# Second pass of expert tiles: the finish moved one turn later, and three list groups marked ahead of the loop

## The chip, the cores and the metric

The kernel runs on one core of a Trainium2 chip. The metric is the device time of one execution in microseconds (us). Engines: TensorE (PE, with its weight loads PEld), VectorE (DVE), ScalarE (ACT), GpSimd (POOL), SyncE (SP); DMA queues are fed by SP and POOL.

## The reference

Cross-attention of 4096 tokens of width 512 on a context of 3202 rows (16 heads), a residual, and then a layer of 8 experts of which each token uses 2. All in float32. The part that matters here:

```
x = x + attention(layernorm(x), ctx, ctx, Wq, bq, Wk, bk, Wv, bv, Wo, bo)
h = layernorm(x)
p = softmax(h @ W_router.T + b_router)            # 4096 x 8
w, e = top_k(p, 2)                                # two experts a token, with weights
x = x + sum over j in (0, 1) of  w[:, j] * (h @ W_experts[e[:, j]].T + b_experts[e[:, j]])
```

## The kernel before

Attention and the router take the first 2055 us of the profiled execution; the change is in what follows, the function mix_experts. The residual rows stand in a DRAM table, token_rows, of 4096 rows with two halves of 516 floats: the near half holds the row, its layernorm scale and shift and the two weights, the far half takes the result of the first pass.

The tokens are sorted by expert into tiles of 128 rows, once by their first expert and once by their second. There are NS = 39 tiles in each of the K = 2 passes, so NT2 = 78 tiles in one loop; tile s is in pass k = s // 39, at place n = s % 39. The rows of a tile all go through one expert, so a tile is one product of 128 x 512 by 512 x 512 in three terms (high and low parts). Since 39 tiles allow for eight partly filled ones, the last tiles of a pass may be short or empty; rows that are left out are skipped by the transfer's bounds.

**The lists.** Which row stands where is found by small products: mark_tiles and mark_lanes (VectorE, L1972 and L1977) mark for a group of four columns of tokens their tile and lane, in two buffers by turns, and find (TensorE, L2081) multiplies them into a bank of PSUM, four matmuls a group. A pass has NGR = 8 groups. The first pass's are done ahead of the loop. The second pass's are done inside it, one group every three turns, and index(1) (L1985 to L1990), which turns them into row numbers, is in turn 28.

**The loop.** Each engine runs its own list of instructions in order; semaphores order them among each other. For tile s:

- GpSimd: scatter(s) waits for finish(s), then writes the result, in pass 0 to the far half of the table (L1898), in pass 1 to the output (L1902). Behind it gather(s + 6) loads the rows of a later tile into one of HOLD = 6 buffers hold: in pass 0 and for the first six tiles of pass 1 the near half alone (L1886), for the others both halves, 128 rows of 4128 bytes (L1890). As a buffer is used again every six tiles, gather(s + 6) waits for finish(s). For the first six tiles of pass 1 the far half is loaded by gather_far (L1910), once every scatter of pass 0 has landed; two of them stand behind the last scatter of pass 0, one behind each gather after that.
- ScalarE: in its iteration s, normal(s + 3) (L1935), which waits for the gather, and behind it high(s + 2) (L1942), which waits for the turned tile.
- TensorE: multiply(s) (L2103), then turn(s + 2) (L2089, four transposes), then in some turns find.
- VectorE: biased(s) (L2003) adds the bias to multiply's result, low(s + 2) (L1994) makes the low part, finish(s) (L2012) multiplies by the weight and adds the rows of hold (near half in pass 0, far half in pass 1), then marks. multiply(s) needs low(s) and high(s). biased(s) needs a free result buffer of RES = 3, so a landed scatter(s - 3).

These are the waits by which the rings turn:

```
pool.wait_ge(final_done, s - HOLD + 1)                 # gather(s)
act.wait_ge(near_in[s % HOLD], 16 * times_used(HOLD, s))  # normal(s)
dve.wait_ge(xh_done, s + 1)                            # low(s), after high(s)
dve.wait_ge(far_in[n], 16)                             # finish(s) in pass 1, n < HOLD
```

Of the kernel before, what the change touches and what calls it, by code (L numbers as in the profile page):

```python
# [1789 lines left out]
def mix_experts(nc, mem, sb0, sem, psum, ident, g, h):  # L1790
    D, KT, NE, L, out = (g[n] for n in "D KT NE L out".split())
    NTL, K, NS, table, we_hi, we_lo, picked, before, mix = (h[n] for n in "NTL K NS table we_hi we_lo picked before mix".split())
    lane, own, mix_stored = (h[n] for n in "lane own mix_stored".split())
    wo = g["wo"]
    G4 = 4
    NGR = NTL // G4
    HOLD, RES = 6, 3
    AHEAD = 2
    MARKS_OVER = 3
    FAR_FIRST = 2  # L1800
    RANK_BANK, COUNT_BANK, PLACE_BANK, T_BANK = 0, 1, 2, 4
    OUT_BANKS = (6, 7, 0, 1)
# [2 lines left out]
    NT2 = K * NS  # L1805
    NSE = NS + NS % 2

    with mem:
# [57 lines left out]
        with nc.Block() as block:  # L1866
# [7 lines left out]
            def _(pool):  # L1874
                def gather(s):
                    k, n = kn(s)
                    if s >= HOLD:
                        pool.wait_ge(final_done, s - HOLD + 1)
                    else:
                        pool.wait_ge(counted, 4 + s + 1)  # L1880
                    if s == 0 or n == 0:
                        pool.wait_ge(indexed, k + 1)
                    if s == 0:
                        pool.wait_ge(mix_stored, 16 * NGR)
                    if k == 0 or n < HOLD:
                        pool.indirect_dma_start(out=hold[s % HOLD][:, 0:ROW], out_offset=None, in_=halves[:, :],  # L1886
                                                in_offset=bass.IndirectOffsetOnAxis(ap=near[k][:, n:n + 1], axis=0),
                                                bounds_check=2 * L - 1, oob_is_err=False).then_inc(near_in[s % HOLD], 16)
                    else:
                        pool.indirect_dma_start(out=hold[s % HOLD][:, :], out_offset=None, in_=table[:, :],  # L1890
                                                in_offset=bass.IndirectOffsetOnAxis(ap=whole[:, n:n + 1], axis=0),
                                                bounds_check=L - 1, oob_is_err=False).then_inc(near_in[s % HOLD], 16)
# [16 lines left out]
                def gather_far(n):  # L1909
                    pool.indirect_dma_start(out=hold[(NS + n) % HOLD][:, ROW:2 * ROW], out_offset=None, in_=halves[:, :],  # L1910
                                            in_offset=bass.IndirectOffsetOnAxis(ap=far[1][:, n:n + 1], axis=0),
                                            bounds_check=2 * L - 1, oob_is_err=False).then_inc(far_in[n], 16)

                for s in range(NT2):
                    scatter(s)
                    if s == NS - 1:
                        for b in range(RES):
                            pool.wait_ge(scattered[b], 16 * len(range(b, NS, RES)))
                        for n in range(FAR_FIRST):
                            gather_far(n)  # L1920
                    if s + HOLD < NT2:
                        gather(s + HOLD)
                    if NS - 1 <= s < NS - 1 + HOLD - FAR_FIRST:
                        gather_far(s - (NS - 1) + FAR_FIRST)
                for b in range(RES):
# [33 lines left out]
            def _(dve):  # L1959
                c = h["chained"]  # L1960

                def step(ins):
                    c[0] += 1
                    ins.then_inc(chain, 1)
                    dve.wait_ge(chain, c[0])
# [16 lines left out]
                def index(k):  # L1982
                    dve.wait_ge(placed, RANKED + (k + 1) * NTL)
                    found = psum[:, PLACE_BANK + k, 0:NS]
                    step(dve.tensor_scalar(gone[:], found, 0.0, SKIPPED, ALU.is_equal, ALU.mult))  # L1985
                    step(dve.scalar_tensor_tensor(out=row_of[:], in0=found, scalar=-1.0, in1=gone[:], op0=ALU.add, op1=ALU.add))
                    if k:
                        step(dve.tensor_copy(whole[:], row_of[:]))
                    dve.tensor_scalar(near[k][:], row_of[:], 2.0, None, ALU.mult).then_inc(indexed, 1)
                    step(dve.tensor_scalar(far[k][:], row_of[:], 2.0, 1.0, ALU.mult, ALU.add))  # L1990
# [15 lines left out]
                def finish(s):  # L2006
                    k, n = kn(s)
                    if k and n < HOLD:
                        dve.wait_ge(far_in[n], 16)
                    dve.wait_ge(bias_done, s + 1)  # L2010
                    rest = hold[s % HOLD][:, ROW:ROW + D] if k else hold[s % HOLD][:, 0:D]
                    dve.scalar_tensor_tensor(out=res[s % RES][:, 0:D], in0=res[s % RES][:, 0:D], scalar=hold[s % HOLD][:, MIX_AT + k:MIX_AT + k + 1], in1=rest,  # L2012
                                             op0=ALU.mult, op1=ALU.add).then_inc(final_done, 1)
# [40 lines left out]
                step(dve.tensor_scalar(expert[:], expert_f[:], float(NE - 1), None, ALU.min))  # L2054
                dve.sem_inc(rankable, 1)
                dve.wait_ge(be_in, 16 * NE)

                for s in range(AHEAD):
                    low(s)
                for s in range(NT2):  # L2060
                    biased(s)
                    if s + AHEAD < NT2:
                        low(s + AHEAD)
                    finish(s)
                    for part in range(s * (G4 + 1) // MARKS_OVER, min((s + 1) * (G4 + 1) // MARKS_OVER, NGR * (G4 + 1))):
                        q, u = divmod(part, G4 + 1)
                        if u == 0:
                            mark_tiles(1, q)
                        else:
                            mark_lanes(1, q, u - 1)  # L2070
                    if s == MARKS_OVER * (NGR + 1) + 1:
                        index(1)

            @block.tensor
            def _(pe):
                def find(k, q):
                    m = k * NGR + q
                    pe.wait_ge(marked, 2 * (m + 1))
                    for u in range(G4):
                        i = q * G4 + u  # L2080
                        pe.matmul(psum[:, PLACE_BANK + k, 0:NSE], at_lane[m % 2][:, u, :], at_tile[m % 2][:, u, :],  # L2081
                                  start=i == 0, stop=i == NTL - 1).then_inc(placed, 1)

                def turn(s):
                    pe.wait_ge(xs_done, s + 1)
                    if s >= 2:
                        pe.wait_ge(xl_done, s - 1)
                    for k in range(KT):
                        mm = pe.transpose(psum[:, T_BANK + s % 2, k * P:(k + 1) * P], xs[s % 2][:, k * P:(k + 1) * P], ident[:])  # L2089
                    mm.then_inc(xs_turned, 1)  # L2090

                def expert_of(s):
                    k, n = kn(s)
                    return pe.value_load(expert[0:1, k, n:n + 1], min_val=0, max_val=NE - 1)

                def multiply(s, e):
                    pe.wait_ge(xh_done, s + 1)
                    pe.wait_ge(xl_done, s + 1)
                    if s >= 4:
                        pe.wait_ge(bias_done, s - 3)  # L2100
                    terms = [(k, A, W) for k in range(KT) for A, W in ((x_hi, we_hi), (x_hi, we_lo), (x_lo, we_hi))]
                    for t, (k, A, W) in enumerate(terms):
                        mm = pe.matmul(psum[:, OUT_BANKS[s % 4], :], A[s % 2][:, k, :], W[:, k, ds(e, 1), :].rearrange("p o n -> p (o n)"),  # L2103
                                       start=t == 0, stop=t == len(terms) - 1)
                    mm.then_inc(e_mm, 1)

                pe.wait_ge(rankable, 2)
                pe.matmul(psum[:, COUNT_BANK, 0:K * NE], all_ones, before[:, NTL].rearrange("p k e -> p (k e)"), start=True, stop=True).then_inc(ranked, 1)
                pe.matmul(psum[:, RANK_BANK, :], earlier, picked[:].rearrange("p i k e -> p (i k e)"), start=True, stop=False)
                pe.matmul(psum[:, RANK_BANK, :], all_ones, before[:, 0:NTL].rearrange("p i k e -> p (i k e)"), start=False, stop=True).then_inc(ranked, 1)  # L2110
                for q in range(NGR):
                    find(0, q)
                pe.wait_ge(rankable, 3)
                for s in range(AHEAD):
                    turn(s)
                for s in range(NT2):
                    e = expert_of(s)
                    multiply(s, e)
                    if s + AHEAD < NT2:
                        turn(s + AHEAD)  # L2120
                    if s >= MARKS_OVER + 2 and (s - 2) % MARKS_OVER == 0 and (s - 2) // MARKS_OVER <= NGR:
                        find(1, (s - 2) // MARKS_OVER - 1)


_DRAM = ["x", "ctxT", "Wq", "bq", "Wk", "bk", "Wv", "bv", "Wo", "bo", "WeT", "be", "WrT", "br"]
# [29 lines left out]
```

## Time and profile before

| | us |
|---|---|
| median of 3 runs | 2355.64 (2354.8 to 2356.03) |
| the profiled execution, its time | 2361.31 |
| the profiled execution, its span | 2358.5 |
| TensorE busy over the span | 2266.8 (96%) |
| VectorE busy | 2035.5 (86%) |
| ScalarE busy | 1840.5 (78%) |
| GpSimd busy | 746.6 (32%) |
| first multiply of the expert loop starts | 2081.91 |
| last scatter starts | 2349.52 |

The expert loop is the last 11% of the span, so the shares over the whole span say little about it; the rows below are from its own stretch.

### The profile page before, as it was taken

What the parts mean: (1) busy time and instruction counts of PE and PEld (TensorE: products, weight loads), DVE (VectorE), ACT (ScalarE), POOL (GpSimd) and SP (SyncE); (2) the same over time, 40 slices, a digit from 0 to 9 for tenths busy, and PEclk for the clock granted to TensorE, in tenths of its full rate; (3) what the DMA queues carried; (4) which work ended last, traced back from release to release, by engine and by line L of the source; (5) the groups of instructions that cost most, each with busy time, mean ns of one, the idle gap of its engine ahead of it and who ended that gap; (6) DMA issues with size and microseconds to landing.
All of it is one profiled execution on the core that took longest, in us unless ns stands there. A gap on an engine that the chain in (4) does not pass through costs nothing. (4 is left out here: it accounts for less than half of the span.)

```text
span 2358.5 us, 49254 instructions
## 1 busy us (share of the span) xinstructions
PE 2266.8 (96%) x19600; PEld 1088.8 (46%) x19600; DVE 2035.5 (86%) x1830; ACT 1840.5 (78%) x2123; POOL 746.6 (32%) x823
## 2 busy tenths in 40 slices
PE   8999799999999999999999999999999999789998
PEld 7878533333333333333333333333333357578776
DVE  4358579999999999999999999999999988866555
ACT  3213299999999999999999999999999956534332
POOL 2213223323223322223323232332233222245664
PEclk9999899999999999999999999999999999889999
DMA  7436463444464455557444535645434467634463
GB/s 261 166 133 224 171 184 91 109 107 107 113 175 108 127 127 131 130 140 208 109 109 115 120 92 129 170 100 120 109 95 106 109 171 267 201 112 139 144 215 120
DMA packets 145020, 334.24 MB, mean 142 GB/s; under 512 B 32758, under 2 KB 65494, under 8 KB 127644
## 3 DMA queue, kind: packets, MB, share of 16 engines
q0 software_dynamic: 47104, 194.30, 33.8%
q1 hardware_dynamic: 95356, 129.20, 16.8%
q10 hardware_dynamic: 2336, 7.60, 1.0%
q8 instruction: 159, 2.61, 0.4%
q14 instruction: 65, 0.53, 0.1%
HBM read 131.16 MB, written 82.78 MB: 91 GB/s over the span
## 5 line engine op out<-in xcount | busy, mean ns | idle before, releaser
L1162 ACT ACTIVATE probs<-psum 128x1536 f32<-128x1536 f32 x800 | 1159.5, 1449 | 0.0
L1316 PE MATMUL psum<-probs,v_st 128*32 128x512 f32 x6400 | 853.9, 606 | 0.2 <-ACT probs L1162 0.2
L1267 PE MATMUL psum<-q_st,k_st 32*128 32x512 f32 x9600 | 781.2, 426 | 28.6 <-ACT probs L1162 13.6
L1267 PEld LDWEIGHTS psum<-q_st,k_st 32*128 32x128 f32 x9600 | 399.0, 184 | 722.8 <-ACT probs L1161 376.3
L1227 DVE TENSOR_TENSOR even_sums<-even_sums,probs 128x2048 f32<-128x2048 f32 x288 | 659.7, 2291 | 39.1 <-ACT probs L1162 36.2
L1227 DVE TENSOR_TENSOR odd_sums<-odd_sums,probs 128x2048 f32<-128x2048 f32 x256 | 585.4, 2287 | 1.6 <-ACT probs L1162 1.6
L1161 ACT ACTIVATE probs<-psum 128x512 f32<-128x512 f32 x800 | 478.2, 598 | 47.3 <-PE psum L1267 42.8
L1316 PEld LDWEIGHTS psum<-probs,v_st 128*32 128x32 f32 x6400 | 126.1, 108 | 291.3 <-issue 281.9
L2103 PE MATMUL psum<-we_hi,wo 128*128 x624 | 216.9, 409 | 4.5 <-DVE wo L1994 2.5
L977 POOL DMA_DIRECT2D pile<-probs x96 | 88.8, 925 | 247.2 <-DMA pile<-probs 156.7
L956 POOL CAST rest_split<-rest_probs 72x512 fp32r<-72x512 f32 x32 | 37.4, 1169 | 386.1 <-ACT rest_probs L1130 386.1
L971 POOL DMA_DIRECT2D pile<-rest_probs x128 | 103.6, 1222 | 149.3 <-DMA pile<-probs 149.3
L1935 ACT ACTIVATE shared_rows<-hold 128x512 f32<-128x512 f32 x78 | 63.5, 814 | 102.3 <-DMA hold<-token_rows,whole 62.4
L2103 PEld LDWEIGHTS psum<-we_hi,wo 128*128 128x128 f32 x624 | 118.2, 189 | 31.5 <-issue 6.3
L344 POOL TENSOR_TENSOR squares<-o_hi 128x512 fp32r<-128x512 f32 (+1 forms) x60 | 60.5, 1017 | 208.3 <-ACT o_hi L382 121.0
L2103 PE MATMUL psum<-we_lo,wo 128*128 x312 | 123.7, 397 | 0.0
L1227 DVE TENSOR_TENSOR even_sums<-probs 128x2048 f32<-128x2048 f32 x32 | 105.7, 3302 | 12.2 <-ACT probs L1162 12.2
L1942 ACT ACTIVATE wo<-psum 128x512 fp32r<-128x512 f32 x78 | 46.0, 590 | 75.5 <-PE psum L2089 75.5
L958 POOL TENSOR_TENSOR rest_split<-rest_probs,rest_split 8x512 fp32r<-8x512 f32 x32 | 100.5, 3141 | 2.7
L1994 DVE TENSOR_TENSOR wo<-psum,wo 128x512 fp32r<-128x512 f32 x78 | 53.9, 691 | 53.2 <-ACT wo L1942 53.1
L762 PE MATMUL psum<-wo,q_st 128*128 128x512 f32 x384 | 96.4, 400 | 0.0
L786 POOL DMA_DIRECT2D shared_rows<-inv_scratch x124 | 61.8, 506 | 88.7 <-DMA inv_scratch<-spread_inv 88.7
(225 smaller groups left out, 2358.9 us busy)
## 6 DMA issues: line engine op xcount, KB each, us to landing
pile<-probs POOLq DMA_DIRECT2D x128, 1024.0 KB, 7.3
token_rows<-rows SPq DMA_DIRECT2D x8, 1028.0 KB, 6.7
xn<-in_x SPq DMA_DIRECT2D x16, 512.0 KB, 6.4
qh_scratch<-o_hi SPq DMA_DIRECT2D x8, 1024.0 KB, 4.5
ql_scratch<-o_lo SPq DMA_DIRECT2D x8, 1024.0 KB, 7.6
q_st<-qh_scratch SPq DMA_DIRECT2D x32, 256.0 KB, 3.0
q_st<-ql_scratch SPq DMA_DIRECT2D x32, 256.0 KB, 3.6
token_rows<-in_x SPq DMA_DIRECT2D x8, 1024.0 KB, 10.7
```

The source lines that it names most:

```text
L762: mm = pe.matmul(psum[:, bank, :], A[:, j, :], W[:, j, :], start=False, stop=t == len(terms) - 1)
L786: pool.dma_start(a["recip"][h * DH:(h + 1) * DH, :], a["inv_d"][h:h + 1, :].to_broadcast([DH, CH])).then_inc(a["inv_in"], 16)
L958: pool.tensor_tensor(rest_split[DH:DH + REST, :], rest_probs[DH:DH + REST, :], rest_split[DH:DH + REST, :].bitcast(F32), ALU.subtract).the ...
L971: pool.dma_start(out=pile[rows, h, :], in_=rest_probs[rows, :], accum_op=ALU.add).then_inc(piled, 16)
L977: pool.dma_start(out=pile[:], in_=probs[:, p_slot(it, t)], accum_op=ALU.add).then_inc(piled, 16)
L1161: act.activation(probs[:, p, 0, :], psum[:, FIRST_BANK, :], ACT.Exp, bias=-WIDEST, scale=SCALE).then_inc(first_done, 1)
L1162: act.activation(probs[:, p, 1:HG, :], psum[:, bank(it, t, 1):bank(it, t, 1) + HG - 1, :], ACT.Exp, bias=-WIDEST, scale=SCALE).then_inc(ex ...
L1227: nc.vector.tensor_tensor(into[:], a, probs[:, p_slot(it, t)], ALU.add).then_inc(added, 1)
L1267: return nc.tensor.matmul(psum[:, bank(it, t, h), :], k_st[rows, part, t * P:(t + 1) * P], q_st[it % 2][rows, of, :], start=start, stop=stop)
L1316: mm = nc.tensor.matmul(psum[h * DH:(h + 1) * DH, bank, :], lhs(h), rhs(h), start=start, stop=stop)
L1935: act.activation(xs[s % 2], r[:, 0:D], ACT.Identity, bias=r[:, SHIFT_AT:SHIFT_AT + 1], scale=r[:, RSTD_AT:RSTD_AT + 1]).then_inc(xs_done, 1)
L2103: mm = pe.matmul(psum[:, OUT_BANKS[s % 4], :], A[s % 2][:, k, :], W[:, k, ds(e, 1), :].rearrange("p o n -> p (o n)"), start=t == 0, stop=t ...
```

## The change

In the first pass VectorE's order within a turn stays biased(s), low(s + 2), finish(s). In turn 39, the first of the second pass, it does no finish, and from turn 40 on it does finish(s - 1); the last tile's finish stands behind the loop. Three of the second pass's eight list groups are marked, and their products done, ahead of the loop, between the expert numbers and the first low or turn; the other five follow inside the loop from turn 0 on, and index(1) moves from turn 28 to turn 19.

```diff
+    EARLY_GROUPS = 3
...
                 dve.wait_ge(be_in, 16 * NE)
+                for q in range(EARLY_GROUPS):
+                    mark_tiles(1, q)
+                    for u in range(G4):
+                        mark_lanes(1, q, u)
...
                     if s + AHEAD < NT2:
                         low(s + AHEAD)
-                    finish(s)
-                    for part in range(s * (G4 + 1) // MARKS_OVER, min((s + 1) * (G4 + 1) // MARKS_OVER, NGR * (G4 + 1))):
-                        q, u = divmod(part, G4 + 1)
+                    if s < NS:
+                        finish(s)
+                    elif s > NS:
+                        finish(s - 1)
+                    for part in range(s * (G4 + 1) // MARKS_OVER, min((s + 1) * (G4 + 1) // MARKS_OVER, (NGR - EARLY_GROUPS) * (G4 + 1))):
+                        q, u = divmod(part + EARLY_GROUPS * (G4 + 1), G4 + 1)
...
-                    if s == MARKS_OVER * (NGR + 1) + 1:
+                    if s == MARKS_OVER * (NGR - EARLY_GROUPS + 1) + 1:
                         index(1)
+                finish(NT2 - 1)
...
                 pe.wait_ge(rankable, 3)
+                for q in range(EARLY_GROUPS):
+                    find(1, q)
                 for s in range(AHEAD):
                     turn(s)
...
-                    if s >= MARKS_OVER + 2 and (s - 2) % MARKS_OVER == 0 and (s - 2) // MARKS_OVER <= NGR:
-                        find(1, (s - 2) // MARKS_OVER - 1)
+                    if s >= MARKS_OVER + 2 and (s - 2) % MARKS_OVER == 0 and (s - 2) // MARKS_OVER <= NGR - EARLY_GROUPS:
+                        find(1, EARLY_GROUPS + (s - 2) // MARKS_OVER - 1)
```

## Rows read from the trace of the kernel before

**Rows 1.** Windows: stretch, length, each engine's busy time, granted clock, DMA share, GB/s.

```profile
2063.00:2073.00 10.00, 8.35 (x32) 7.43 (x32) 8.86 (x37) 0.00 (x0) 0.00 (x0) 0.50 0.24 90
2079.00:2082.00 3.00, 2.29 (x9) 1.52 (x9) 0.69 (x1) 2.41 (x4) 2.39 (x3) 0.50 0.52 119
2223.00:2230.00 7.00, 5.25 (x28) 4.09 (x27) 5.27 (x8) 1.30 (x2) 5.47 (x6) 1.00 0.67 207
2242.00:2246.00 4.00, 2.78 (x14) 1.78 (x12) 0.64 (x2) 1.30 (x2) 2.42 (x3) 1.00 0.84 276
2246.00:2300.00 54.00, 53.33 (x260) 43.23 (x261) 33.35 (x51) 21.42 (x33) 32.59 (x32) 1.00 0.67 209
```

**Rows 2.** Chain that ended last, in two stretches of the loop: start, length, what.

```profile
2100.24 2.81 PE psum L2103 x12
2103.84 2.90 PE psum L2103 x12
...
2286.28 2.81 PE psum L2103 x12
2289.52 2.81 PE psum L2103 x12
```

**Rows 3.** Timeline at the border of the passes: finish(39), multiply(42), low(44).

```profile
2223.13 0.75 DVE L2012 SCALAR_TENSOR_TENSOR shared_rows<-shared_rows,hold 128x512 f32<-128x512 f32 x1 [4.57 <-DMA hold<-token_rows,far]
...
2225.45 0.49 PE L2103 MATMUL psum<-we_hi,wo 128*128 x1 [1.75 <-issue]
...
2232.26 0.69 DVE L1994 TENSOR_TENSOR wo<-psum,wo 128x512 fp32r<-128x512 f32 x1 [2.90 <-ACT wo L1942]
```

**Rows 4.** Timeline of the second pass: one round from finish(45) to finish(48), then finish(60).

```profile
2246.05 0.74 DVE L2012 SCALAR_TENSOR_TENSOR shared_rows<-shared_rows,hold 128x512 f32<-128x512 f32 x1
...
2247.62 1.00 POOL L1902 DMA_INDIRECT out<-shared_rows,whole  x1 [2.59 <-DVE shared_rows L2012]
...
2248.93 1.03 POOL L1890 DMA_INDIRECT hold<-token_rows,whole  x1 [0.30 <-issue]
...
2253.26 0.82 ACT L1935 ACTIVATE shared_rows<-hold 128x512 f32<-128x512 f32 x1 [2.81 <-DMA hold<-token_rows,whole]
...
2253.99 0.58 ACT L1942 ACTIVATE wo<-psum 128x512 fp32r<-128x512 f32 x1
...
2254.59 0.69 DVE L1994 TENSOR_TENSOR wo<-psum,wo 128x512 fp32r<-128x512 f32 x1 [1.14 <-ACT wo L1942]
...
2255.20 0.74 DVE L2012 SCALAR_TENSOR_TENSOR shared_rows<-shared_rows,hold 128x512 f32<-128x512 f32 x1
...
2295.21 0.74 DVE L2012 SCALAR_TENSOR_TENSOR shared_rows<-shared_rows,hold 128x512 f32<-128x512 f32 x1
```

**Rows 5.** Line L1890, all 33 gathers; timeline: gather(77) and normal(77).

```profile
DMA to landing us min/median/max: 2.1/4.6/5.9
...
2333.04 1.03 POOL L1890 DMA_INDIRECT hold<-token_rows,whole  x1 [0.30 <-issue]
...
2335.52 0.81 ACT L1935 ACTIVATE shared_rows<-hold 128x512 f32<-128x512 f32 x1
```

**Rows 6.** Timeline ahead of the loop: marks and matmuls of pass 0, expert numbers, turn(0).

```profile
2061.67 0.33 DVE L1972 TENSOR_TENSOR wo<-lane,tile_of 128x160 fp32r<-128x160 f32 x1
...
2062.94 0.32 DVE L1972 TENSOR_TENSOR wo<-lane,tile_of 128x160 fp32r<-128x160 f32 x1
...
2063.07 1.04 PE L2081 MATMUL psum<-wo 128*128 128x40 f32 x4 [5.70 <-DVE wo L1977]
...
2075.77 0.19 DVE L2054 TENSOR_SCALAR expert<-expert_f 1x78 int32<-1x78 f32 x1
...
2079.05 1.09 PE L2089 MATMUL psum<-ident,shared_rows 128*128 128x128 f32 x4 [6.10 <-ACT shared_rows L1935]
```

**Rows 7.** Timeline at the end: first matmul of multiply(76), and scatter(77).

```profile
2341.24 0.48 PE L2103 MATMUL psum<-we_hi,wo 128*128 x1
...
2349.52 0.98 POOL L1902 DMA_INDIRECT out<-res,whole  x1 [1.82 <-DVE res L2012]
```

## The prediction

> **What bounds the kernel now.** The change touches only the expert stage, so I read the windows of that stage first, then the chain that ended last, then the timeline at three places: the start of the loop, the border between the two passes, and the steady part of the second pass. I write F(s), B(s), L(s), H(s), N(s), T(s), M(s) for finish, biased, low, high, normal, turn and multiply of tile s, S(s) and G(s) for its scatter and gather; tiles 39 to 77 are the second pass.
>
> The windows say that TensorE is the busiest engine in the loop: 53.33 of 54 us between 2246 and 2300, at full clock, against 33.35 for VectorE and 32.59 for GpSimd [rows 1]. The chain agrees: M to M takes 2289.52 - 2286.28 = 3.24 us, and a turn in the first pass that also holds a group of list matmuls takes 2103.84 - 2100.24 = 3.60, so one group costs 0.36 [rows 2]. The reader should see, though, that at the border the engine is not full: 5.25 of 7 us and 2.78 of 4 [rows 1]. There F(39) waits 4.57 us on VectorE for its far half, and TensorE shows an idle 1.75 us before M(42), because L(42) is queued behind F(39) [rows 3]. This is the wait that moving the finish goes at.
>
> The view that decides is none of the totals. It is one round through the ring of six row buffers. G(s+6) may start only after F(s), since it overwrites the rows that F(s) reads. N(s+6) waits for it to land. ScalarE issues N(s+6) ahead of H(s+5), so H(s+5) waits too; L(s+5) follows H(s+5). The timeline shows all of it for tile 45: F(45) 2246.05, S(45) 2247.62, G(51) 2248.93, N(51) 2253.26, H(50) 2253.99, L(50) 2254.59, and right behind it on VectorE F(48) 2255.20 [rows 4]. The steps are 1.57 + 1.31 + 4.33 + 0.73 + 0.60 + 0.61 = 9.15 us. In the order of before, L(50) and F(48) stand in the same turn, so a round carries the finishes three tiles on: 9.15 / 3 = 3.05 us a tile, only 0.19 under TensorE's 3.24. From F(45) to F(60), 15 tiles, it took 2295.21 - 2246.05 = 49.16, or 3.28 a tile [rows 4]. Two resources thus stand side by side, and TensorE's share of busy time hides the second.
>
> **The change, part by part.**
>
> *The finish one turn later.* In turn s of VectorE the order is now B(s), L(s+2), F(s-1). L(50) is in turn 48, and what stands behind it is F(47), not F(48). The round of 9.15 us, none of whose links is touched, now carries the finishes two tiles on: F(s+2) is at least F(s) + 9.15. That is 4.58 us a tile against 3.24, as two interleaved chains, even and odd. It is the late gather that is paid for: S(s), G(s+6) and everything behind them on GpSimd's queue wait a turn longer.
>
> Does anything cover it? TensorE needs 3.24 a tile and can't run ahead, as M(s+2) needs L(s+2). GpSimd needs S and G, 2 x 1.31 = 2.6. The wait of B(s) for the landed S(s-3) is the shorter path beside it, since the path through G also has the longer transfer. So nothing hides it while gathers are still to come, which means up to G(77), released by F(71) and ending in F(73).
>
> Where the rounds begin: at the border F(39) still waits for the same far gather until 2223.13, and GpSimd's three transfers a turn run as before, so L(44) stays near 2232.26 [rows 3]. I take F(41) = 2232.26 + 0.61 = 2232.87. M(42) may start earlier by the 1.75, but M(44) waits for L(44) all the same, so I cost this gain at nothing; if it were kept it would be -1.75. From F(41) to F(73) are 16 rounds: 16 x 9.2 = 147.2 (9.15 rounded up for the waits at GpSimd). The last gathered tile is short: G(77) starts 2333.04 and N(77) runs at 2335.52 without a wait, so 2.48 at most instead of 4.4 [rows 5], which takes off 1.9. F(73) = 2232.9 + 147.2 - 1.9 = 2378.2. L(76) stands 0.61 ahead of it, 2377.6, and M(76) 0.9 behind L(76) (0.69 of VectorE and some 0.2 until TensorE starts), 2378.5. Before, M(76) started at 2341.24 [rows 7]: +37.2 us. Behind it the tail is as before, but F(76) and F(77) are now back to back and S(77) queues behind S(76): one more slot of 1.31. Sum of this part: **+38.5**.
>
> The landing is the term that I know least. Over the 33 whole-row gathers it is 2.1 / 4.6 / 5.9 us, least, median, most [rows 5]; the round above has 4.33. With the median it would be 16 x 0.27 = 4.3 more. Against that, the queues carry one tile in 4.6 us rather than 3.24, so crowding eases. I take 4.33 to 4.4, that of a gather with no other right ahead of it, and keep -0.6 and +0.7 a round for the range (-10, +11).
>
> The Trainium skill, page "DMA: Bandwidth & Descriptors", section "Anatomy of one DMA — SWDGE (gpsimd) path", gives 2.0 us plus the bytes over 436 GB/s for such a transfer. For 128 rows of 4128 bytes this is an estimated 3.2 us, and by it this part would be near 16 x 1.13 = 18 us smaller; the row at 4.33 disagrees, and the sum goes by the row.
>
> *Three groups marked ahead of the loop.* The work on the expert numbers ends at 2075.77 + 0.19 + 0.04 = 2076.0. A group of marks takes 2062.94 - 2061.67 = 1.27 us, and its matmuls start 1.40 behind its first mark [rows 6]. The third group starts at 2078.54, its matmuls at 2079.94, and four of them took 1.04, so they end at about 2080.9. VectorE is free by 2079.9, in time for L(0). But T(0) started at 2079.05 [rows 6] and is queued behind these matmuls on TensorE: +1.85 at the start of the loop. The pause isn't as long as it looks from VectorE. In the loop three groups go, 3 x 0.36 = -1.07. VectorE has slack in those turns, and the earlier index(1) is needed by no one before tile 39; both nothing. Sum: **+0.8**. The clock bounds it: at 2079 to 2082 it is granted at 0.50, the 1.2 GHz level, and 8.35 us of work in 2063 to 2073 did not raise it [rows 1]. If the later start lets M(0) run more of its work at the 2.4 GHz level, up to 2 us come back; so +0.8, from -1.3 to +1.0.
>
> **Sum.** 38.5 + 0.8 = +39.3 us. The rows are from one execution with a span of 2358.5 us and a time of 2361.31; the median of the runs is 2355.64. On the median: 2355.64 + 39.3 = **2395 us**.
>
> **The rivals.**
>
> *The ring has slack, and the border's wait is saved.* If the ring were no limit, the result would be 1.85 - 1.07 - 1.75 = -1.0, so 2354.7; with the clock's 2 us back, 2352.7. For it speaks the full TensorE of 2246 to 2300. It decides if a round fits in two turns of TensorE, 2 x 3.24 = 6.49 us, so only if a gather landed in 4.33 - 2.66 = 1.67 us, under the least landing of 2.1 [rows 5]. Chance 0.05. It is the only case on the faster side, and even it stays mostly within 0.2% (4.7 us), about what a measurement of this kernel can tell.
>
> *The gathers land sooner once the queues are emptier.* Halfway between 2.48 and 4.33 the landing is 3.4, 0.93 less: 16 x 0.93 = 15, so 2380 us. Against it: gathers with little ahead of them, as G(51), still took 4.33. Chance 0.08. The page's 3.2 us above would give about 2377.
>
> *TensorE's clock falls.* It would be idle for 4.6 - 3.24 = 1.3 us a turn. At the lower level a turn would take 6.49, so 32 x (6.49 - 4.58) = 61 more: 2456. But at the border it was busy for 5.25 of 7 and 2.78 of 4 us, 70 to 75% and so much as it would be then (3.24 / 4.58 = 71%), and the clock stayed at 1.00 [rows 1]. Chance 0.05.
>
> *The forecast*, 2384 to 2408: chance 0.82. Its own bounds are 2395 - 10 - 2 = 2383 and 2395 + 11 = 2406; I widen the top by 2, for parity chains that meet at GpSimd. Leaving out the three rivals leaves out under 2 in 10, so that is the range. Faster 0.02, within 0.2% 0.04, slower 0.94.
>
> **What would show each step.** Right: in the timeline of the second pass F(s+2) - F(s) of about 9.2 us with L(s+5) just ahead of F(s+2), TensorE at some 70% from 2235 to 2380 and idle before its turns or multiplies with ScalarE's rows waiting for the whole-row gather; a gather after each scatter, a turn later than before; T(0) near 2080.9; 3.60 us turns five times, not eight; two scatters back to back at the end. Wrong: TensorE full in the second pass, or a landing well off 4.4 us, which scales the result sixteenfold; or a granted clock of 0.50 beyond tile 0.

## The result and the profile after

The changed kernel takes 2396.07 us (median of 5 runs, 2394.09 to 2396.74) against 2356.03 (5 runs, 2354.8 to 2359.08) of the kernel before beside it: 40.0 us more, a ratio of 1.0165 with a 95% interval of 1.0151 to 1.0178, which is 35.6 to 41.9 us. The prediction was +39.3 us.

The page of the changed kernel, its span and its first part (busy time and share of the span):

```profile
span 2392.7 us, 49254 instructions
PE 2279.1 (95%) x19600; PEld 1092.5 (46%) x19600; DVE 2034.0 (85%) x1830; ACT 1840.1 (77%) x2123; POOL 747.3 (31%) x823
```

No engine got more work: each runs as many instructions as before. VectorE, ScalarE and GpSimd are busy for the same time as before within 2 us. TensorE shows 12 us more for the same matmuls, since a multiply or a turn that starts after a pause takes longer (3.06 us in place of 2.81 for a multiply's twelve, see below). The loss is idle time, and nothing on this page says where. (The two spans differ by 34.2 us only, since the part ahead of the expert stage, which the change does not touch, was 4.1 us shorter in this execution. I compare from the operation on the expert numbers on.)

The windows of the changed kernel, columns as in [rows 1]:

```profile
2160.00:2210.00 50.00, 50.00 (x249) 40.75 (x248) 31.07 (x46) 21.50 (x31) 31.05 (x32) 1.00 0.40 127
2235.00:2380.00 145.00, 119.51 (x518) 86.67 (x516) 63.79 (x98) 40.79 (x63) 64.61 (x63) 0.98 0.44 143
2260.00:2264.00 4.00, 4.00 (x11) 3.03 (x10) 1.08 (x2) 0.00 (x0) 3.09 (x4) 0.50 0.43 125
```

In the first pass TensorE is full. In the second it is busy for 119.51 of 145 us, where before it was busy for 53.33 of 54 [rows 1]. VectorE is at 44%, GpSimd at 45%, the queues at 0.44: nobody is busy enough to be the bound. That is how a chain of waits looks in a table of busy times.

One round in the timeline of the changed kernel, from finish(52) to finish(54), which answers to [rows 4]:

```profile
2281.41 0.74 DVE L2013 SCALAR_TENSOR_TENSOR res<-res,hold 128x512 f32<-128x512 f32 x1
...
2282.99 1.01 POOL L1903 DMA_INDIRECT out<-res,whole  x1 [2.62 <-DVE res L2013]
...
2284.30 1.03 POOL L1891 DMA_INDIRECT hold<-token_rows,whole  x1 [0.30 <-issue]
...
2288.72 0.81 ACT L1936 ACTIVATE shared_rows<-hold 128x512 f32<-128x512 f32 x1 [3.57 <-DMA hold<-token_rows,whole]
2289.44 0.58 ACT L1943 ACTIVATE wo<-psum 128x512 fp32r<-128x512 f32 x1
...
2290.05 0.69 DVE L1995 TENSOR_TENSOR wo<-psum,wo 128x512 fp32r<-128x512 f32 x1 [2.92 <-ACT wo L1943]
2290.66 0.74 DVE L2013 SCALAR_TENSOR_TENSOR shared_rows<-shared_rows,hold 128x512 f32<-128x512 f32 x1
```

The steps are 1.58, 1.31, 4.42, 0.72, 0.61 and 0.61, 9.25 us, against 9.15 before [rows 4]: the same links. But the finish behind low(57) is that of tile 54, two tiles on from 52, and not three. The far ends of the stretch, finish(41) and finish(73):

```profile
2229.33 0.74 DVE L2013 SCALAR_TENSOR_TENSOR res<-res,hold 128x512 f32<-128x512 f32 x1
...
2374.00 0.74 DVE L2013 SCALAR_TENSOR_TENSOR res<-res,hold 128x512 f32<-128x512 f32 x1
```

That is 144.67 us for 32 tiles, 4.52 us a tile; as 16 rounds, 9.04 each in the mean. (The rounds are not alike: the section on why the prediction was right takes them apart.) The line of the whole-row gathers (L1891) answers to [rows 5], and says who paid:

```profile
who waited for it (us, times):
  ACT shared_rows L1936: 106.7, 33
...
DMA to landing us min/median/max: 2.1/4.3/5.8
```

All 33 gathers are waited for, before it was 62.4 us over 30 of them. The landing is little changed, 4.3 against 4.6 us in the median. The transfer isn't slower; it is asked for later.

### The profile page after: what moved, and what is told of

Read it like the earlier page. It is cut to its first block and busy times, and to the rows that moved or that the text cites. A ratio compares the mean times of both kernels' runs of the same rounds, so it can differ in the third digit from the quotient of the medians.

```text
span 2392.7 us, 49254 instructions
## 1 busy us (share of the span) xinstructions
PE 2279.1 (95%) x19600; PEld 1092.5 (46%) x19600; DVE 2034.0 (85%) x1830; ACT 1840.1 (77%) x2123; POOL 747.3 (31%) x823
## 5 line engine op out<-in xcount | busy, mean ns | idle before, releaser
L956 POOL CAST rest_split<-rest_probs 72x512 fp32r<-72x512 f32 x32 | 37.8, 1181 | 383.4 <-ACT rest_probs L1130 383.4
```

## The experiments

Each time stands beside runs of the kernel before on the same chip. Those runs had medians of 2358 to 2364 us from one chip to the next, so the ratio counts, not the bare time, and a difference given with a ratio is the ratio's share of the median before.

**The change in its two halves.** First the late finish alone, and then the early groups alone.

```diff
-    EARLY_GROUPS = 3
+    EARLY_GROUPS = 0
```

> The finish one turn later alone; all eight list groups in the loop as before. Ring theory (a gather waits for the finish six tiles back, and low and the next finish wait for that gather): all of the loss but 0.8 us is here, +38.5 us on before (35 to 42), finishes of every second tile 9.2 us apart. Rival, that the marks ahead of the loop carry a good part of the loss (a later start and a slower clock at tile 0): clearly less, under +30.

Measured: 2395.21 us against 2359.82, ratio 1.016 (1.0144 to 1.0175), which is +37.8 us.

```diff
-                    if s < NS:
-                        finish(s)
-                    elif s > NS:
-                        finish(s - 1)
+                    finish(s)
...
-                finish(NT2 - 1)
```

> Three groups marked ahead of the loop alone; the finish in its old turn. Ring theory and the sum of the prediction: +1.85 us at the first multiply, -1.07 for three groups in the loop, so +0.8 us (-1.3 to +1.0 by the clock). Rival, that marks done in the pause are free: -1.1 us.

Measured: 2359.92 against 2359.82 us, ratio 1.0001 (0.9991 to 1.0011), so +0.2 us within 2.4. The late finish is all of the loss that can be measured. The +0.8 and the rival's -1.1 can't be told apart by the total, but the trace has what the argument rested on. The timeline of this kernel, the third early group's matmuls, the turns and the first multiply:

```profile
2077.77 1.04 PE L2086 MATMUL psum<-wo 128*128 128x40 f32 x4 [0.24 <-DVE wo L1978]
2078.65 1.97 PE L2094 MATMUL psum<-ident,shared_rows 128*128 128x128 f32 x8
2081.37 0.79 PE L2108 MATMUL psum<-we_hi,wo 128*128 x1 [0.76 <-DVE wo L1995]
```

The turns have no idle time in front of them: they stand behind the early group's matmuls and not behind their rows, as turn(0) did before [rows 6]. The first multiply starts 7.96 us after the operation on the expert numbers (2073.41 in this trace), before 6.14 us (2075.77 to 2081.91). So the pause was not free.

**Seven row buffers, with the change and without it.** The seventh lies over the arrays picked and picked_before, which are dead by then; ScalarE clears it once the ranks are read.

```diff
-    HOLD, RES = 6, 3
+    HOLD, RES = 7, 3
...
-    picked = sb("picked", [P, NTL, K, NE], F32R)
-    before = sb("picked_before", [P, NTL + 1, K, NE], F32R)
+    both = sb("picked_both", [P, (2 * NTL + 1) * K * NE], F32R)
+    picked = both[:, 0:NTL * K * NE].rearrange("p (i k e) -> p i k e", k=K, e=NE)
+    before = both[:, NTL * K * NE:].rearrange("p (i k e) -> p i k e", k=K, e=NE)
...
-        hold = [sb(f"hold{b}", [P, 2 * ROW], F32) for b in range(HOLD)]
+        hold = [sb(f"hold{b}", [P, 2 * ROW], F32)[:] for b in range(HOLD - 1)] + [h["both"][:, 0:2 * ROW].bitcast(F32)]
...
+                    if b == HOLD - 1:
+                        act.wait_ge(marked, 1)
```

> The changed kernel with seven row buffers in place of six (the seventh lies over two arrays that are dead by then); nothing else. Ring theory: a gather is released a tile sooner, so a round of 9.15 us carries the finishes three tiles on again, 3.05 us a tile, under TensorE's 3.24: nearly all of the loss gone, 2352 to 2360 us. Rival, the three result buffers (biased waits for a scatter that starts a turn later, and the changed kernel's trace has 5.6 us of such waits): the buffers of rows don't matter, and it stays over 2380 us. Rival, TensorE's clock: falls only with idle time, so gone too with the first theory.

Measured: 2358.79 against 2359.82 us, ratio 0.9999 (0.999 to 1.0008). With the late finish still in place, one more buffer takes away the whole loss. The three result buffers were not what cost 40 us. They are next in line, though. The next run has the same seven buffers without the late finish and takes 2355.54 us, so beside that one the late finish still costs some 3 us, little more than the intervals of the two runs. The line of biased in this kernel:

```profile
  PE psum L2115: 40.8, 43
  DMA out<-shared_rows,whole: 26.0, 11
  DMA out<-res,whole: 25.8, 18
```

VectorE now waits 51.8 us for landed scatters, over 29 tiles, against 4.0 + 1.6 us in the changed kernel. This is the path that the prediction put beside the other: finish(s - 3), scatter(s - 3), its landing, biased(s). (The profiled execution took 2364.58 us, 5.8 more than the median, so its waits may be on the high side.)

> The kernel before with seven row buffers. Ring theory: four tiles a round, 2.3 us a tile; the small unevenness of the second pass (3.28 against 3.24 us a tile, some 1 us in all) goes, and at the border of the passes one more tile's rows are there ahead of the far gathers, which may give back part of the 6.7 us that ten tiles lose there: -1 to -5 us. Rival, that the ring costs nothing before: 0.

Measured: 2355.54 against 2359.82 us, ratio 0.9985 (0.9976 to 0.9994), so -3.5 us (-5.7 to -1.4). Most of the gain is at the border and just behind it. At the same distance from the operation on the expert numbers (2209.4 to 2244.4 here, 2211 to 2246 before) TensorE is busy for 32.14 of 35 us against 30.32, and in the next 35 us for 34.88 against 34.33: 2.4 us less idle time. Where the rest comes from was not traced.

**Four result buffers in the changed kernel.** The fourth takes the free end of shared_rows, made 32 bytes longer in each partition; one small scratch array is shared to make room.

```diff
-        shared_rows = sb("shared_rows", [P, 4, CH], F32)
+        shared_all = sb("shared_rows", [P, 4 * CH + 8], F32)[:]
+        shared_rows = shared_all[:, 0:4 * CH].rearrange("p (n c) -> p n c", n=4)
...
-        total = sb("total", [P, G4], F32)
+        total = tmp
...
-    HOLD, RES = 6, 3
+    HOLD, RES = 6, 4
...
+        res = [rows_flat[:, 2 * D:2 * D + ROW]] + [sb(f"res{b}", [P, ROW], F32)[:] for b in range(1, RES - 1)] + [rows_flat[:, 2 * D + ROW:2 * D + 2 * ROW]]
```

> The changed kernel with four result buffers in place of three, six row buffers as before. Ring theory: the chain through gather, normal, high and low is the longer one, so the waits of biased for a landed scatter (5.6 us in the changed kernel's trace) lie beside it: within 4 us of the changed kernel, 2392 to 2397 us. Rival, that the later scatter is what costs: most of the loss gone.

Measured: 2392.45 against 2358.32 us, ratio 1.0144 (1.0129 to 1.016), +34.0 us. The waits of biased for scatters are gone from the trace, and the loss stays. Its interval, 30.4 to 37.7 us, overlaps that of the changed kernel, 35.6 to 41.9, so the few us between them may be noise. One small cause is shown by the last run: where the arrays lie. In the first pass, where no buffer is waited for, finishes are 3.20 us apart in this kernel and 3.25 in the other kernels on the same chip.

**The dose: two turns late.**

```diff
-                    elif s > NS:
-                        finish(s - 1)
+                    elif s > NS + 1:
+                        finish(s - 2)
...
+                finish(NT2 - 2)
                 finish(NT2 - 1)
```

> The changed kernel with the finish two turns late in place of one (finish of tile s - 2 in turn s, the last two behind the loop). Ring theory: a round of 9.15 us carries the finishes one tile on, so 9.2 us a tile for some 31 tiles against 3.24: about +185 us on before, 2530 to 2550 us. A rival in which a later finish costs a fixed lag of one turn each (3.24 us), or in proportion to the turns (twice 39 us): 2362 or 2434 us.

Measured: 2553.12 us in one run, +194.8 on 2358.32. Four finishes running in its timeline:

```profile
2300.59 0.74 DVE L2013 SCALAR_TENSOR_TENSOR res<-res,hold 128x512 f32<-128x512 f32 x1
...
2309.76 0.74 DVE L2013 SCALAR_TENSOR_TENSOR shared_rows<-shared_rows,hold 128x512 f32<-128x512 f32 x1
...
2318.82 0.74 DVE L2013 SCALAR_TENSOR_TENSOR res<-res,hold 128x512 f32<-128x512 f32 x1
...
2327.84 0.74 DVE L2013 SCALAR_TENSOR_TENSOR res<-res,hold 128x512 f32<-128x512 f32 x1
```

9.17, 9.06 and 9.02 us from one tile to the next. The second turn of lateness costs 155 us where the first cost 40: neither a fixed lag nor in proportion, but the same round divided by one in place of two. The time is 3 us above the range that I expected. The kernel before was itself 2.7 us slower on this chip than the 2355.64 from which the prediction starts, which is about as much. This kernel's granted clock is down to 0.71 over 2240 to 2500; whether that costs anything was not tried.

**The same division by another way: five row buffers, and no late finish.**

```diff
-    HOLD, RES = 6, 3
+    HOLD, RES = 5, 3
```

> The kernel before with five row buffers and the finish in its old turn. Ring theory: the round carries two tiles on here too, without any late finish: 4.6 us a tile in the second pass (some 33 tiles, +44 us), and in the first pass, where half rows land in a median 3.4 us, about 8.2 / 2 = 4.1 us a tile (some 33 tiles, +28 us): near +72 us, 2420 to 2440 us. Rival, that the late finish hurts by something of its own (order on VectorE, late scatters) and not by the ring: little loss here.

Measured: 2428.38 us in one run, +67.1 on 2361.28. Finishes in the timeline of its second pass:

```profile
2312.29 0.74 DVE L2012 SCALAR_TENSOR_TENSOR res<-res,hold 128x512 f32<-128x512 f32 x1
...
2321.50 0.74 DVE L2012 SCALAR_TENSOR_TENSOR shared_rows<-shared_rows,hold 128x512 f32<-128x512 f32 x1
...
2330.63 0.74 DVE L2012 SCALAR_TENSOR_TENSOR res<-res,hold 128x512 f32<-128x512 f32 x1
```

There is one finish between each two of these, so two tiles take 9.21 and 9.13 us, as in the changed kernel, with the old order on VectorE. In the second pass a turn of lateness and a buffer less are the same loss. But the missing buffer acts in the first pass too, where the change had left the order alone. This is its finish(39), which stood at 2223.13 before [rows 3]:

```profile
2251.12 0.75 DVE L2012 SCALAR_TENSOR_TENSOR shared_rows<-shared_rows,hold 128x512 f32<-128x512 f32 x1 [4.84 <-DMA hold<-token_rows,far]
```

Counted from the operation on the expert numbers it starts after 177.07 us in place of 147.36, 29.7 us later (expected: 28). From there to the last scatter it is another 40.0 us more than before, the loss of the changed kernel. So of this kernel's loss of 67 us only the second part is to be compared with the 40.

**ScalarE's order turned,** with the change and without it.

```diff
+                    high(s + AHEAD)
                     if s + AHEAD + 1 < NT2:
                         normal(s + AHEAD + 1)
-                    high(s + AHEAD)
```

> The changed kernel with ScalarE's order turned: high(s + 2) ahead of normal(s + 3). Ring theory: high no longer waits for the next tile's gather, so a round is 1.57 + 1.31 + 4.33 + 0.82 (normal) + 0.66 (turn) + 0.6 (high) + 0.6 (low), and 0.2 between them, 10.1 us for three tiles: 3.37 us a tile, 0.13 over TensorE's 3.24: +4 us over 32 tiles and +1 at the start, 2357 to 2364 us. Rival, the gather's own lateness with any order of ScalarE: stays over 2380 us.

Measured: 2367.02 against 2358.32 us, ratio 1.0034 (1.0022 to 1.0046), +8.0 us. Turning two instructions of ScalarE, which do the same work, gives back four fifths of the loss. So the link from normal to high is one of the round. The rest is more than the +5 of my sum, and 3 us over the top of my range for it. From finish(41) to finish(73) it is 117.09 us, 3.66 a tile where the sum had 3.37. One link was sized too small. These are normal(59) and the turn behind it:

```profile
2281.69 0.82 ACT L1936 ACTIVATE shared_rows<-hold 128x512 f32<-128x512 f32 x1 [0.80 <-DMA hold<-token_rows,whole]
...
2283.36 0.60 PE L2098 MATMUL psum<-ident,shared_rows 128*128 128x128 f32 x4
```

The turn starts 1.67 us behind the start of normal, not 0.82, since TensorE is still in a multiply; this round, from finish(53) at 2274.56 to finish(56) at 2285.24, takes 10.68 us and not 10.1. In this trace biased also waits 12.4 + 6.6 us for landed scatters, nine times, which the sum left out; how the difference divides between the two was not tried.

> The kernel before with high(s + 2) ahead of normal(s + 3). Ring theory: 10.1 us for four tiles, so the second pass loses its small unevenness, and at the border the multiply of tile 44 no longer stands behind normal(45): -1 to -5 us. Rival, that the border is set by GpSimd's transfers whatever the order: 0.

Measured: 2358.93 against 2358.32 us, ratio 0.9999 (0.999 to 1.0008): nothing. I had expected 1 to 5 us at the border and in the second pass. The theory says where a round is too long and not what a shorter one gives where TensorE is the bound.

**Seven row and four result buffers on the kernel before,** and the same with ScalarE's order turned. To free a semaphore for them, rankable also counts what indexed did.

> The kernel before with seven row buffers and four result buffers. With seven row buffers alone biased waited at the border for landed scatters (1.3 to 1.7 us a turn); if these waits were on the path, another -1 to -4 us on the -3.6 us of the seven row buffers: 2350 to 2354 us against 2356 to 2359 of before. If they lie beside the gathers, the same as with three.

Measured: 2350.68 against 2361.28 us, ratio 0.9958 (0.9944 to 0.9971), -9.9 us. This version beats both kernels.

> As the run before, with high(s + 2) ahead of normal(s + 3) on ScalarE. Alone this order gave nothing; if the border's order of rows and multiplies matters once the rings have slack, -1 to -3 us on the run before; else 0.

Measured: 2351.56 against 2361.28 us, ratio 0.9958 (0.9944 to 0.9971). The order gives nothing here either.

The gain was more than twice what I had expected, and its trace had something that no buffer explains: TensorE's turn was shorter in the first pass too, where nothing had waited. The chain in the kernel before has starts of multiplies 3.24 us apart [rows 2]. So the last run is the kernel before with its arrays moved by the same 32 bytes, and three result buffers:

```diff
-        shared_rows = sb("shared_rows", [P, 4, CH], F32)
+        shared_all = sb("shared_rows", [P, 4 * CH + 8], F32)[:]
+        shared_rows = shared_all[:, 0:4 * CH].rearrange("p (n c) -> p n c", n=4)
...
-        total = sb("total", [P, G4], F32)
+        total = tmp
```

> The kernel before with the array shared_rows 32 bytes longer in each partition, so that the arrays allocated behind it lie 32 bytes further on, and one small scratch array shared to make room; both are part of the runs with four result buffers, whose traces show 3.20 us a turn of TensorE against 3.24. Theory, that the place of the arrays in SBUF sets this: 3.20 us a turn here too, 78 turns, -3 to -4 us, so some third of the gain of seven row and four result buffers is this and not the buffers. Rival, that the fourth result buffer does it: 3.24 us a turn and no change.

Measured: 2360.25 against 2363.63 us, ratio 0.9982 (0.9973 to 0.9991), -4.3 us. The chain of this kernel:

```profile
2179.56 2.76 PE psum L2104 x12
2182.32 0.44 PE psum L2090 x4
2182.76 2.76 PE psum L2104 x12
2185.52 0.44 PE psum L2090 x4
2185.96 2.76 PE psum L2104 x12
```

3.20 us from one multiply to the next, and 2.76 us for its twelve matmuls where the kernel before has 2.81 [rows 2]. (The profiled execution took 2364.4 us, 4.2 more than the median, with the granted clock at 0.85 over 2211 to 2246, so I read only its first pass.) Of the 9.9 us, then, some 4.3 come from where the arrays lie, some 3.5 from the seventh row buffer, and what is left, about 2, may be the fourth result buffer. The three runs were on three chips and each of these numbers has an interval of 2 us or more to either side, so this last term is not shown.

## Why the prediction was right

The mechanism was the one that the prediction named, and the experiments leave it without a rival: one more row buffer takes the loss away, a fourth result buffer does not, one more turn of lateness divides the same round by one, and one buffer less gives the same rounds with the old order. That the sum came within 1 us of the measured 40.0 is in part luck, as the rounds show.

From the operation on the expert numbers to the last scatter, the profiled executions have 273.75 us before and 2383.72 - 2071.66 = 312.06 after, +38.3. Step by step:

- **The start.** Predicted +1.85 us until the first multiply. Measured 7.96 against 6.14 us, +1.82. The clock gave almost nothing back: the multiply of tile 0 takes 4.84 us in the chain, 4.92 before, both with most of it at the granted 0.50. Groups in the loop: five turns of 3.60 us in place of eight, as predicted.
- **To finish(41).** The prediction's times give 2232.87 - 2081.91 - 1.07 = 149.9 us from the first multiply. Measured 2229.33 - 2079.62 = 149.7. So the 1.75 us that the border's wait cost TensorE [rows 3] came back and was lost again, as costed: there is no pause before multiply(42), but TensorE stands idle for 0.52, 0.70, 0.42 and 0.70 us before the next two turns and the two multiplies behind them. Finish(39) itself waited 1.38 us in place of 4.57 [rows 3]: the edit did what it says.
- **The rounds.** Predicted 147.2 - 1.9 = 145.3 us for 16, measured 144.67. Two errors cancel in this. Finishes 67, 69 and 71 of the chain that ends in finish(73):

```profile
2350.47 0.74 DVE L2013 SCALAR_TENSOR_TENSOR res<-res,hold 128x512 f32<-128x512 f32 x1
...
2359.56 0.74 DVE L2013 SCALAR_TENSOR_TENSOR shared_rows<-shared_rows,hold 128x512 f32<-128x512 f32 x1
...
2366.64 0.74 DVE L2013 SCALAR_TENSOR_TENSOR res<-res,hold 128x512 f32<-128x512 f32 x1
```

  Up to finish(69) the 14 rounds took 130.23 us, 9.30 each and not 9.2, so 1.4 us more than predicted; one of them alone took 10.67, behind gather(51), which landed late. The last two took 7.08 and 7.36 us, so 2.1 us less: the prediction took one gathered tile for short, but each of gathers 74 to 77 was 2.1 to 2.6 us from its start to its normal. The trace of the kernel before had a second one to see, gather(76), at 2.45 us.
- **The tail.** The last three rows of VectorE and GpSimd:

```profile
2380.89 1.41 DVE L2013 SCALAR_TENSOR_TENSOR res<-res,hold 128x512 f32<-128x512 f32 x2
2382.43 0.98 POOL L1903 DMA_INDIRECT out<-res,whole  x1 [0.87 <-DVE res L2013]
2383.72 0.98 POOL L1903 DMA_INDIRECT out<-res,whole  x1 [0.30 <-issue]
```

  Two finishes and two scatters back to back, 1.29 us for the second; predicted 1.31.

Two further details were off, at no cost to the sum. I said that TensorE would be busy for some 70% of the second pass, and it was 82% (119.51 of 145). I had divided the full stream's 3.24 by 4.58 us. A multiply that starts after a pause takes 3.06 us in the chain of the changed kernel and a turn 0.66, 3.72 in all, which over 4.52 is 82%; a stream hides these ends. And the clock's rival did come true, for one tile:

```profile
2257.11 0.66 PE L2098 MATMUL psum<-ident,shared_rows 128*128 128x128 f32 x4 [2.82 <-ACT shared_rows L1936]
...
2258.55 0.79 PE L2112 MATMUL psum<-we_hi,wo 128*128 x1 [0.79 <-DVE wo L1995]
```

Gather(51) took 5.85 us to land, TensorE stood idle for 2.82 us and again for 0.79, and the granted clock fell to 0.50, the 1.2 GHz level, in 2260 to 2264. The next multiply took 5.3 us until the next turn. It cost nothing that can be seen: the finishes of tiles 46 and 48 are 9.39 us apart and those of 47 and 49 9.33, an ordinary round, since TensorE had the slack. In the run with the late finish alone the clock fell two times, again for a short while, to 0.57 over 2275 to 2279 and over 2340 to 2344, after idle times of 1.12 and 0.70 us, and of 0.95 and 0.70. So the prediction's reading of the border, that the clock would stay up at such a load, did not hold throughout. The rival's price of 61 us held only for a clock that stays down.

The estimate from the Trainium skill ("DMA: Bandwidth & Descriptors", "Anatomy of one DMA — SWDGE (gpsimd) path"), 3.2 us for such a transfer, is not what the traces have: 4.3 us in the median here, at a queue share of 0.44, and 4.42 in the round above. The sum with the row's 4.33 was the right one.

## What to carry to other kernels

Where a ring of buffers is refilled by a load that waits for the last reader, add up one round from reader to reader, and divide it by the number of tiles that it carries on. That number is the count of buffers less everything that runs ahead and every turn of lateness, so a turn's delay can change the divisor from three to two while each single step stays as fast as it was. (Here it is six buffers less three, and less one more in the changed kernel.) A busy engine at 99% doesn't show how near the second bound is: here it was 0.19 us a tile away.

Before moving a step later in an in-order engine, list everyone who waits for it, and not only what it waits for. And before filling a pause on one engine, look at whose queue the other half of the work stands in.

## What the runs showed of the hardware that I had not expected

Arrays that lie 32 bytes further on in SBUF made TensorE's twelve matmuls of a multiply take 2.76 us in place of 2.81, and the kernel 4.3 us faster (ratio 0.9982, 0.9973 to 0.9991), with no instruction of TensorE changed. All three other kernels with the moved arrays have turns 3.19 to 3.20 us apart, and none of the unmoved ones that I looked at, moved and unmoved on one chip among them. Over 78 turns 0.045 us each is an estimated 3.5 of the 4.3 us. Which array's place matters was not tried, nor the shared scratch array by itself. A difference of some us between two versions of a kernel that also move its arrays is therefore no evidence for either.
